# The adjacency spill of a two-layer graph convolution, laid out in blocks of 1568 bytes by partition

## What is computed

```
def gcn_conv(x, W, b, src, dst, n):
    h = x @ W
    ...
    deg = jax.ops.segment_sum(ones, d, num_segments=n)
    dis = jnp.where(deg > 0, jax.lax.rsqrt(jnp.maximum(deg, 1e-12)), 0.0)
    norm = dis[s] * dis[d]
    msgs = h[s] * norm[:, None]
    out = jax.ops.segment_sum(msgs, d, num_segments=n)
    return out + b
...
g = jax.nn.relu(gcn_conv(service_emb, W1, b1, src, dst, NUM_SERVICES))
g = gcn_conv(g, W2, b2, src, dst, NUM_SERVICES)
ctx = g[context_idx].reshape(context_idx.shape[0], -1)
x = jnp.concatenate([user_vec, ctx], axis=1)
return x @ fc_W + fc_b
```

## Time and profile before

| | us |
|---|---|
| median of three executions | 767.07 (767.07 to 769.0) |
| the profiled execution | 769.29 |
| its span in the profile | 767.5 |
| PE busy | 600.2 (78%) |
| DVE busy | 600.4 (78%) |
| ACT busy | 423.3 (55%) |

### The profile page before, as it was taken

How to read it: one execution, slowest core, us unless ns; L and a number is a source line. 1 busy time by engine, 2 the same in 40 slices (tenths; PEclk the granted TensorE clock), 3 DMA queues, 4 the chain that set the end, 5 groups by cost and what they waited for, 6 DMA issues and landing times.

```text
span 767.5 us, 21867 instructions
## 1 busy us (share of the span) xinstructions
PE 600.2 (78%) x9504; PEld 563.7 (73%) x9504; DVE 600.4 (78%) x1436; ACT 423.3 (55%) x770; POOL 178.6 (23%) x181
## 2 busy tenths in 40 slices
PE   0453657747657755578699999999999999998897
PEld 0343657747657854478699999999999999998543
DVE  9999999999999999786999999999982211111386
ACT  4996188889879311357588888888877000000000
POOL 1100000020000000577766666666100000000500
PEclk9967779799778875589899999999999999999999
DMA  7000000000000000245366665556000999859376
GB/s 128 2 1 1 1 1 1 1 5 2 1 4 1 2 0 1 72 112 177 120 204 210 210 200 196 193 207 210 13 3 23 417 415 399 286 132 274 90 306 284
DMA packets 39143, 94.13 MB, mean 123 GB/s; under 512 B 19097, under 2 KB 21843, under 8 KB 39044
## 3 DMA queue, kind: packets, MB, share of 16 engines
q1 hardware_dynamic: 24340, 74.28, 26.3%
q0 software_dynamic: 5216, 9.91, 6.0%
q10 hardware_dynamic: 9488, 8.52, 3.5%
HBM read 48.50 MB, written 44.18 MB: 121 GB/s over the span
## 4 chain that ended last, share of the span: by engine, by line
PE 52%; DVE 37%; issue 3%; ACT 3%; POOL 2%; DMA 2%; SPq 0%; DVEq 0%; POOLq 0%
PE pp L1431 17%; PE pp L1449 14%; PE psY L1449 13%; DVE arena L962 12%; DVE arena L963 12%; PE pp L1550 6%; DVE arena L949 3%; POOL arena L656 2%; ACT arena L713 2%; PE pp L1367 1%; DMA arena<-ordered_keys,window 1%; DVE arena L957 1%; DVE arena L958 1%; PE psX L1418 1%; DVE arena L960 1%
## 5 line engine op out<-in xcount | busy, mean ns | idle before, releaser
L656 POOL DMA_INDIRECT arena<-ordered_keys,window x147 | 157.3, 1070 | 217.9 <-DMA ordered_keys<-arena 147.5
L790 ACT ACTIVATE arena<-pp 128x512 uint16<-128x512 f32 x308 | 172.0, 584 | 43.5 <-PE pp L1431 41.2
L1431 PE MATMUL pp<-arena 128*128 128x128 fp8e4 (+1 forms) x2401 | 189.4, 221 | 7.7 <-DVE arena L1141 7.7
L713 ACT ACTIVATE arena<-arena,neg_word 128x780 fp8e4<-128x780 bf16 (+1 forms) x200 | 170.1, 945 | 0.0
L1431 PEld LDWEIGHTS pp<-arena 128*128 128x128 fp8e4 (+1 forms) x2401 | 148.3, 98 | 8.2 <-issue 6.2
L1449 PE MATMUL psY<-arena 128*128 128x96 bf16 x2401 | 150.6, 207 | 2.7 <-ACT y_s L774 2.6
L1449 PEld LDWEIGHTS psY<-arena 128*128 128x128 fp8e4 x2401 | 123.4, 98 | 2.9 <-ACT arena L790 2.7
L1140 DVE TENSOR_SCALAR arena<-arena 128x384 int32<-128x384 int32 (+5 forms) x224 | 111.0, 496 | 7.4 <-PE pp L1431 7.3
L1449 PE MATMUL pp<-arena 128*128 128x96 bf16 x2401 | 105.8, 207 | 8.2 <-issue 8.2
L1449 PEld LDWEIGHTS pp<-arena 128*128 128x128 fp8e4 x2401 | 104.3, 99 | 9.8 <-issue 9.7
L962 DVE TENSOR_TENSOR arena<-arena 128x832 f32<-128x832 f32 (+4 forms) x121 | 107.5, 888 | 3.9 <-ACT arena L736 1.1
(11 more groups left out here) (205 smaller groups left out, 518.8 us busy)
## 6 DMA issues: line engine op xcount, KB each, us to landing
arena<-adjacency_spill SPq DMA_DIRECT2D x32, 784.0 KB, 10.5
adjacency_spill<-arena SPq DMA_DIRECT2D x24, 768.0 KB, 4.0
adjacency_spill<-arena SPq DMA_DIRECT2D x8, 832.0 KB, 4.0
out_dram<-arena SPq DMA_DIRECT2D x12, 512.0 KB, 2.6
out_dram<-arena ACTq DMA_DIRECT2D x8, 512.0 KB, 2.9
arena<-adjacency_spill SPq DMA_DIRECT2D x8, 392.0 KB, 4.8
arena<-ordered_keys,window POOLq DMA_INDIRECT x147
arena<-in_L_rec_fc_b_dram SPq DMA_DIRECT2D x3, 784.0 KB, 12.2
```

What stands on the lines that cost most here:

```text
L656: nc.gpsimd.indirect_dma_start(gath[:, k, q, :], None, ordered, bass.IndirectOffsetOnAxis(ap=window[:, q, d:d + 1], axis=0)).then_inc(gat[ ...
L713: ins = nc.scalar.activation(cols8[n % BUFS][:, 4 * u:4 * u + 4, 0:c1 - c0], high4[:, :, c0:c1], ACT.Sign, bias=neg_word[:, u:u + 1], satu ...
L790: nc.scalar.mul(adj16[g % SLOTS][:, m0 * P:m1 * P], bank(gp)[:, 0:(m1 - m0) * P], PAIR_SCALE).then_inc(evicted, 1)
L1431: ins = MM(bank(gp)[:, (n - n0) // 2 * P:((n - n0) // 2 + 1) * P], src_hot(h, n - a), dst_hot(h, n - a), start=n % 2 == 0, stop=n % 2 == 1 ...
```

## The change

The spill tensor becomes group, block, partition, bytes. A group of c chunks has 4 c blocks, each of 1568 bytes a partition (1600 for the one-chunk group); DMA k of a group, out and back, carries blocks k c to (k + 1) c - 1. In SBUF a partition's bytes stay where they were, contiguous; in DRAM consecutive blocks of a partition lie 128 x 1600 bytes apart, and consecutive partitions of a block 1600 bytes. A store now waits for the pairs that cover its blocks: for a full group 7, 13, 19 and 25 of 25 in place of 6, 12, 18 and 25. Loads are cut in the same four parts as stores.

```diff
-LOAD_PARTS = 4
+BLOCKS_MAX, BLOCK_MAX = 4 * GC, (NH + 1) * P // 4
...
+def block_of(g):
+
+    return -(-bytes_of(g) // (16 * chunks_of(g))) * 4
+
+
+def blocks_of(g, part):
+
+    return range(part * chunks_of(g), (part + 1) * chunks_of(g))
...
-    spill = nc.dram_tensor("adjacency_spill", (NG, P, SLOT_BYTES), U8).ap()
+    spill = nc.dram_tensor("adjacency_spill", (NG, BLOCKS_MAX, P, BLOCK_MAX), U8).ap()
...
+        def spill_part(g, part, slot):
+            m, e = blocks_of(g, part), block_of(g)
+            tile = at(adj_at[slot] + m.start * e, len(m) * e, U8).rearrange("p (m e) -> p m e", e=e)
+            return spill[g, m.start:m.stop, :, 0:e].rearrange("m p e -> p m e"), tile
...
             for g in range(NSPILL):
                 for k in range(SPILL_PARTS):
-                    a, b = (pairs_of(g) * n // SPILL_PARTS for n in (k, k + 1))
-                    c, e = (min(n * PAIR // 2 * 2 * P, bytes_of(g)) for n in (a, b))
-                    sp.wait_ge(evicted, pairs_before(g) + b)
-                    sp.dma_start(spill[g, :, c:e], at(adj_at[g % SLOTS] + c, e - c, U8)).then_inc(spilled[g % SLOTS], 16)
+                    sp.wait_ge(evicted, pairs_before(g) + min(pairs_of(g), -(-blocks_of(g, k).stop * block_of(g) // (PAIR * P))))
+                    sp.dma_start(*spill_part(g, k, g % SLOTS)).then_inc(spilled[g % SLOTS], 16)
...
-                    part = -(-bytes_of(ORDER[i]) // LOAD_PARTS)
-                    for c in range(0, LOAD_PARTS * part, part):
-                        w = min(part, bytes_of(ORDER[i]) - c)
-                        sp.dma_start(at(adj_at[place2[i]] + c, w, U8), spill[ORDER[i], :, c:c + w]).then_inc(loaded[place2[i]], 16)
+                    for k in range(SPILL_PARTS):
+                        stored_part, chip_part = spill_part(ORDER[i], k, place2[i])
+                        sp.dma_start(chip_part, stored_part).then_inc(loaded[place2[i]], 16)
...
-                        pe.wait_ge(loaded[place2[i]], 16 * LOAD_PARTS * (i // 5 + (1 if i % 5 >= 3 else 0)))
+                        pe.wait_ge(loaded[place2[i]], 16 * SPILL_PARTS * (i // 5 + (1 if i % 5 >= 3 else 0)))
```

## The result

Five executions of the changed kernel have a median of 771.35 us (769.46 to 772.48) against 767.12 for the kernel before: ratio 1.0058, 95% interval 1.0031 to 1.0086. A second series on another chip (the first experiment) gave 1.0016 (0.9990 to 1.0043). Both weighted alike, that is 1.0037, between 1.0018 and 1.0056: 1.4 to 4.3 us slower. The forecast was 2.0 us slower.

A forecast was written before the change was run, and what follows sets the result against it. PE was taken as the bound, in layer 2 also waiting for its own instructions. From a median of 767.07 us: stores 0, loads 0, fetch +2.0, run-up 0, giving 769.1 us; range 762 to 772.

The forecast's parts named there:

- Packet price: Spill DMAs: 0.067 us per 1568-byte packet, 374 GB/s instead of 416, 11% more for a 6272-byte row.
- Stores, loads against PE: Layer 1 stores stay covered by PE's 20.05 us a group; layer 2 loads land in time, 22 us of cover: 0.
- The break point: Layer 2: loads come late for PE only under 280 GB/s; rival that they fall behind: 775 us, chance 0.08.
- Issue cost: SP issuing spill DMAs: no added cost, 0.43 us for 128 packets against ACT's 0.40 for the context table's 512.
- SP's 63.7 us: Layer 2 before the change: SP's loads wait 63.7 us in nine waits for PE to free a slot.
- Fetch of instructions: Layer 2: spill loads delay PE's instruction fetch; fuller queue makes gaps 12 x 0.60 = 7.2 us for 5.2, +2.0 us.
- both rivals that set on a shorter queue: Layer 2 fetch: packet count decides, ten gaps go, 761.9 us, chance 0.22; shorter turn, 0.17 off each, 765.4, chance 0.12.
- The boundaries near 643 and 661: Layer 2: two points where PE had no instruction gap before; each was forecast to get one of 0.60 us.
- The +4.3: Layer 2 instruction gaps: upper end of the fetch term if packets cost 4.5% more, in place of +6.8 at 11%.
- Run-up: 330 to 370 us, a store just ahead of a 4.31 us key gather: between -1.5 and +0.5 us, taken as 0.

The follow-up runs named there:

- the first experiment: The changed kernel, unedited, measured again on another chip: ratio 1.0016 to the kernel before; layer 2 took 117.02 us.
- e1: The changed kernel with its DRAM order and later store waits, but one block per DMA, so 6272-byte packets: ratio 1.0011 to the kernel before, layer 2 114.63 us.
- e6_before: The kernel before with 41 instead of 36 filler matmul pairs ahead of the dense layer: ratio 0.9983, layer 2 113.07 us.
- e0: The changed kernel, unedited, run again on another chip: ratio 1.0016 to the kernel before, layer 2 117.02 us, tail 12.76 us.
- e2: The kernel before, its layout and stores kept, with only the spill loads cut into 1568-byte packets: ratio 1.0017, layer 2 117.49 us.
- e6_after: The changed kernel with 41 instead of 36 filler matmul pairs ahead of the dense layer: ratio 1.0009 to the kernel before, layer 2 117.46 us.
- e7_8x4: The kernel before with spill groups loaded in eight DMAs, at most four in flight: ratio 1.0051, layer 2 104.07 us.
- e7_8x3: The kernel before with spill groups loaded in eight DMAs, at most three in flight: ratio 1.0263, layer 2 121.3 us.
- e3: The kernel before without layer 2's spill loads, PE multiplying what lies in the slots instead: ratio 0.9912, layer 2 107.82 us.
- e4_392: The changed kernel with blocks of 392 bytes instead of 1568: ratio 1.0666 to the kernel before, layer 2 122.0 us.
- e4_784: The changed kernel with blocks of 784 bytes instead of 1568: ratio 1.0065 to the kernel before, layer 2 118.35 us.

## Why the prediction was right, and where not

**Sign and size.** 769.1 us was forecast from a median of 767.07, 1.0026; the two series together give 1.0037 (1.0018 to 1.0056). Layer 2 grew by 2.1 us in the profiled pair, and by 3.0 over seven traces: 114.3 on the mean of before, e1 and e6_before (113.1 to 115.3), 117.4 of after, e0, e2 and e6_after (117.0 to 117.5). Not all of this need reach the end: from layer 2's last sum to the end of the span the former take 57.9 to 60.9 us, the latter 57.8 to 59.3. That the forecast came within a microsecond is in part luck: its one term was forecast too large, and a stage that the sum left out, the tail, made up for it.

**Packet price.** Right: 0.067 us forecast, 0.066 measured; 374 GB/s forecast, 376 for SP's queue from 595 to 640 us in after (385 for all queues, where before has 416). Four packets of 66 ns stand for one of 239: 10% more by these medians, 12% by the means (68 and 243), where 11% was worked out from the rows. The Trainium skill's "DMA: Bandwidth & Descriptors", section "Why small descriptors are slow", would have given 4.5%; these runs don't agree with it.

**Stores, loads against PE.** Right: 20.05 us a group, and no wait of PE for a load. The break point holds up: at 318 GB/s on SP's queue no such wait (e7_8x4), at 270 it is there (e7_8x3).

**Issue cost.** Wrong in the row, harmless in the time. The row taken for 512 packets, the context table's, was from a queue with room, where the stores of after take 0.36 us as well; for a load of 512 packets behind others of its kind an issue holds SP 1.45 us. The price of an issue has to be read from a queue as full as the one it will meet. The wait for a slot hid it, which the prediction had in hand as SP's 63.7 us and did not use.

**Fetch of instructions.** The mechanism was right as far as the loads go: e3 shows that they make the gaps, e2 that the small loads change them, and both rivals that set on a shorter queue fall: the gaps neither vanish nor shrink by 0.17 us each. That the delay goes by bytes or time holds from 6272 to 784 bytes (3.4 to 4.0 us while the queue is full; in each of the three traces with large rows one fetch near 640 us starts after 2.9 to 3.2, and no gap follows it). It does not hold at 392 bytes (e4_392, 0.7 to 3.2 us), and with four loads in flight no fetch comes late. What exactly a fetch waits for stays open. The Trainium skill's rule of turns, "DMA: Bandwidth & Descriptors", section "Queues, rings and completion order", may hold for the turns themselves; 3.4 to 4.0 us is not one turn of a row, 0.24 us at most. The size was off: 12 x 0.60 = 7.2 us was forecast, 5.2 to 5.5 us in ten or eleven came. The boundaries near 643 and 661 that had no gap got one (644.1 and 662.4), as forecast, and the last one, at 673, lost its own. But a gap did not rise to 0.60: it is 0.50 on the mean (5.5 / 11), with single ones from 0.33 to 0.72 while the queue is full. The prediction took two gaps of a full queue for all of them, and the smaller ones for the sign of a queue running empty; but the kernel before has 0.33 to 0.46 as well between 600 and 640 us, where its queue is at 98%. Over the seven traces this term is 5.3 - 4.4 = +0.9 us, not +2.0; the kernel before's 5.2 was the highest of its kind (4.1 and 3.8 in the others). The +4.3 that the prediction has for an upper end at 4.5% is a slip of the sum: 12 x (0.60 + 0.16) - 5.2 is +4.0 before rounding.

**The tail.** What made up for it was not in the sum: the 20 us before the end of layer 2, beside the dense layer's loads. The tail is 11.0 us on the mean with large packets and 12.6 with small ones, +1.6. Of that, 1.1 is the wait ahead of the last 59 matmuls (2.7 us on the mean with small packets; 0.21, 2.08 and 2.63 with large ones), and 0.5 the clock: a stretch at the low clock, 1.6 us, is in six of the seven tails, in all but e6_before_run41's. It lies on the last 59 matmuls in all four traces with loads of 1568 bytes, but also in e1 with large ones, and not in e4_784, where smaller packets still are loaded. So that the packets cause the longer tail is not shown; it may go by when the last fetches fall. Nor does standing still bring the low clock by itself. The end of layer 2 in e6_before_run41, from its chain:

```profile
697.29 2.63 issue
699.92 2.68 PE pp L1449 x59
```

PE stands still for as long as in after, and the 59 matmuls take 2.68 us and not 4.28.

Of the 3.0 us, 0.9 is gaps and 1.6 the tail; 0.2 more is the wait ahead of the tail (1.8 us on the mean for 1.6). The last 0.3 goes with the number of gaps: 128 matmuls between two gaps take 5.60 us, but 5.47 where they run on (after, 639 without a gap):

```profile
668.16 27.32 PE pp L1461 x639
```

The small packets have two more such breaks on the mean, at 0.13 us each.

**Run-up.** Nothing to see in the pair: the first full group of layer 1 starts at 370.42 us before and 370.46 after, though the gather of 4.31 us is no longer on the chain. Between executions of these kernels that point moves from 367 to 374 us (377 at 392 bytes). Over the seven traces it spreads by 5.4 us, as much as their spans (763.6 to 769.0 us).

## What to carry to other kernels

A stream of large DMAs can cost an engine that is short of nothing else through its instructions: look for idle time marked "issue" at a fixed number of instructions, and for when the instruction queue's packet starts. Cutting packets four ways is cheap as long as the queue's rate stays above what the reader takes, and that break point can be worked out ahead and found by holding loads back. A stage's gain counts only when its successor is ready: 11 us won in layer 2 were lost whole behind the transfers that the pacing had moved.

## What the runs showed of the hardware

- Four loads of 392 KB in flight gave 332 GB/s over all queues (595 to 640 us) and no instruction gap; a full queue 416 GB/s and 3.8 to 5.2 us of gaps. With three it is 280 GB/s (600 to 645 us), and PE waits for data. Between four and the full queue nothing was run, so where the gaps set in is not shown.
- Beside a full queue of packets of 6272 to 784 bytes, most fetches of PE's instructions start 3.4 to 4.0 us after PE has gone on, and PE stops for 0.2 to 0.9 us; beside 392-byte packets they start after 0.7 to 3.2 us, and PE runs on.
- Stored packets fall off a cliff between 784 and 392 bytes: layer 1's stores, which with the gathers took 0.64 of the DMA engines at 1568 bytes, filled them at 392, at 44 ns a packet on the mean, where one of 784 bytes takes 41 and one of 1568 bytes 70.
- A queue holds its issuer up: 0.43, 1.45, 2.29 and 2.87 us for a load's issue at 6272, 1568, 784 and 392 bytes, behind others of its kind. Stores of the same numbers of packets, four to a group of layer 1, take 0.32 to 0.36 us (medians), even at 392 bytes, where the DMA engines are full.
- A 1.2 GHz stretch of PE costs 1.6 us over 59 matmuls. In the one trace where it falls ahead of a fetch that is late anyway, the kernel before, it lengthened nothing: the tail takes 10.07 us, and 10.88 in e6_before_run41, which has no such stretch.
